# Passage from the cross-attention to the feed-forward of a decoder block: first unit's products inside the drain, later norms and weight splits behind it

## What is computed

```python
x = x + attn(_layernorm(x))            # stage A: differential attention, window 64
x = x + xattn(_layernorm(x), ctx_512)  # stage B: attention to a context, 16 heads
x = x + ffn(_layernorm(x))             # stage C: shared MLP + 16 experts, top 6

# stage C
shared_out = silu_and_mul(xf @ shared_w1.T) @ shared_w2.T
probs = softmax(xf @ gate_w.T)
routing_weights, selected = top_k(probs, 6)
combine = zeros((T, E)).at[arange(T)[:, None], selected].add(routing_weights)
act = silu_and_mul(einsum('th,eoh->teo', xf, w1))
out = einsum('te,tei,ehi->th', combine, act, w2) + shared_out
```

## Time and profile before

| | us |
|---|---|
| three runs | 1419.23, 1417.41, 1419.37 |
| median | 1419.23 |
| the profiled execution: its own time | 1418.07 |
| the profiled execution: span | 1416.2 |
| TensorE busy in the span | 1343.2 (95%) |
| TensorE granted clock, mean | 0.981 |

### The profile page before, as it was taken

The page is one execution under the profiler, slowest core; times in us unless marked ns, Lnnn a source line. Parts: engine busy times, 40 slices in busy tenths (PEclk is TensorE's granted clock), DMA queues, the critical chain, the costliest instruction groups (busy, mean ns, idle before and its releaser), DMA issues.

```text
span 1416.2 us, 28178 instructions
## 1 busy us (share of the span) xinstructions
PE 1343.2 (95%) x10072; PEld 1038.7 (73%) x10072; DVE 850.3 (60%) x1985; ACT 678.0 (48%) x2705; POOL 471.1 (33%) x466
## 2 busy tenths in 40 slices
PE   5899999999999888999999999978999999999998
PEld 4677777877777665576675676646888888888887
DVE  7878778777787666656555655754544343343433
ACT  2676666676666653434444444463333232332322
POOL 3222113112122124545435434551034253443522
PEclk9999999999999989999999999987999999999999
DMA  6011001100011200100101001001026225253230
GB/s 209 23 24 39 16 17 41 29 16 16 16 25 51 75 1 1 72 1 10 63 1 45 27 1 57 1 1 56 32 47 151 42 84 114 41 130 66 46 103 30
DMA packets 29685, 64.59 MB, mean 46 GB/s; under 512 B 6784, under 2 KB 12032, under 8 KB 28288
## 3 DMA queue, kind: packets, MB, share of 16 engines
q1 hardware_dynamic: 29568, 63.05, 16.4%
HBM read 52.42 MB, written 2.23 MB: 39 GB/s over the span
## 4 chain that ended last, share of the span: by engine, by line
PE 72%; issue 12%; DVE 6%; POOL 4%; ACT 4%; DMA 2%; SPq 1%; POOLq 0%; DVEq 0%; ACTq 0%
PE ps L514 30%; PE ps L877 9%; PE ps L800 4%; PE ps L696 4%; PE ps L629 4%; PE ps L661 3%; PE ps L790 3%; PE ps L774 3%; PE ps L782 2%; PE ps L672 2%; POOL ea L1617 2%; PE ps L652 2%; DMA cw<-comb_d 1%; PE ps L569 1%; PE ps L625 1%
## 5 line engine op out<-in xcount | busy, mean ns | idle before, releaser
L1746 POOL TENSOR_TENSOR sg<-sg,cw 128x512 f32<-128x512 f32 x88 | 113.6, 1291 | 278.0 <-ACT sg L1553 268.1
L1357 ACT ACTIVATE pt<-ps 128x512 f32<-128x512 f32 x128 | 76.8, 600 | 245.8 <-PE ps L645 132.0
L1331 DVE TENSOR_TENSOR hh<-ps,sg 128x512 f32<-128x512 f32 x100 | 69.2, 692 | 181.3 <-POOL sg L1746 164.9
L1390 ACT ACTIVATE ea<-ps,negmax 128x64 f32<-128x64 f32 (+1 forms) x512 | 165.4, 347 | 6.0 <-DVE negmax L1083 6.0
L1357 ACT ACTIVATE hhh<-hh 128x512 fp32r<-128x512 f32 x100 | 63.2, 632 | 207.7 <-DVE hh L1331 207.7
L514 PE MATMUL ps<-xnh,wch 128*128 128x512 f32 x400 | 159.4, 399 | 0.5 <-DVE x_sb L1044 0.5
L514 PE MATMUL ps<-xnh,wcl 128*128 128x512 f32 x400 | 159.3, 398 | 0.0
L514 PE MATMUL ps<-xnl,wch 128*128 128x512 f32 x400 | 158.3, 396 | 0.0
L1130 DVE TENSOR_TENSOR qcs<-ps,tabb 128x512 f32<-128x512 f32 x192 | 123.5, 686 | 56.0 <-PE ps L514 55.7
L1617 POOL TENSOR_TENSOR ea<-ea,rden 128x128 f32<-128x128 f32 (+1 forms) x128 | 62.3, 508 | 246.8 <-DVE rden L1039 246.8
L1624 POOL TENSOR_TENSOR eb<-eb,rsum 128x512 f32<-128x512 f32 x64 | 66.7, 1042 | 173.5 <-DVE rsum L1170 173.5
(11 more groups left out here) (148 smaller groups left out, 3436.8 us busy)
## 6 DMA issues: line engine op xcount, KB each, us to landing
raw_w<-in_rawb_dram SPq DMA_DIRECT2D x4, 2432.0 KB, 9.4
kva<-ktmp SPq DMA_DIRECT2D x64, 128.0 KB, 2.3
cw<-comb_d SPq DMA_DIRECT2D x32, 256.0 KB, 5.0
raw_w<-in_rawc_dram SPq DMA_DIRECT2D x4, 1920.0 KB, 7.9
cw<-comb_d SPq DMA_DIRECT2D x16, 224.0 KB, 4.4
raw_a<-in_wqk_dram SPq DMA_DIRECT2D x4, 768.0 KB, 4.8
cw<-comb_d SPq DMA_DIRECT2D x16, 192.0 KB, 6.3
cw<-comb_d SPq DMA_DIRECT2D x16, 160.0 KB, 5.6
```

Source lines behind the costliest of these rows:

```text
L1331: dve.tensor_tensor(hh[:, par, :], bank(C_U[par]), sg[:, par, :], ALU.mult).then_inc(c_h, 1)
L1357: return act.activation(dst, src, ACT.Copy)
L1390: last = act.activation(dst(m, h), src, ACT.Exp, bias=negmax[:, par, i:i + 1], accum_out=sums[:, par, i:i + 1])
L1746: pool.tensor_tensor(sg[:, par, :], sg[:, par, :], cw[:, c % 2, t, :], ALU.mult).then_inc(c_hs, 1)
```

## The change

The first stage C step's gate product moves into drain 1, ahead of the value product, and its up product behind the output product of drain 1 (new functions `c_gate`, `c_up`, cut out of `c_unit`). Norm 9's transposes move from unit 12 to the end of unit 14, norm 10's from drain 0 to step k = 1, norm 11's from k = 0 to k = 3. On DVE the statistics of norm 10 move ahead of an `add_x` in unit 15, `ln_low(9)` to drain 0, `ln_norm(10)` from drain 0 to drain 1, `ln_norm(11)` behind the hidden features of k = 0, and the low halves of norms 10 and 11 to k = 2 and 4. The splits of tiles 3 and 4 move on ACT from unit 15 to k = 8 and 9, and on POOL behind the norms. The logits move from k = 2, 4 to k = 4, 5 and the routing steps on DVE and ACT from k = 2 to 6 to k = 4 to 7. SP's program is the same in both.

```diff
@@ -410,4 +410,3 @@
         B_EXTRA = {("final", 12, 0): [("ln", 8, 0, 2), ("ln", 8, 1, 3)],
-                   ("final", 12, 1): [("ln", 9, 0, 7), ("ln", 9, 1, 2)],
-                   ("drain", 0, 2): [("ln", 10, 0, 2), ("ln", 10, 1, 3)]}
+                   ("final", 14, 2): [("ln", 9, 0, 7), ("ln", 9, 1, 3)]}
@@ -738,4 +737,2 @@
                         if what[0] == "ln":
-                            if what[1:3] == (9, 1):
-                                pe.wait_ge(ln_h, 2 * 8 + 1)
                             if what[1] == 8:
@@ -744,4 +741,3 @@
                                 pe.wait_ge(b_qs, NG * NC)
-                            if drain:
-                                pe.wait_ge(ln_h, 2 * 9 + 2)
+                                pe.wait_ge(ln_h, 2 * 8 + 2)
                             ln_turn(*what[1:])
@@ -788,2 +784,4 @@
                     wait(pe, b_ol, n - 2)
+                    if drain and u == 1:
+                        c_gate(0, 0, 0, 0)
                     for i in range(2):
@@ -802,2 +800,4 @@
                     last.then_inc(b_wo, 1)
+                if drain and u == 1:
+                    c_up(0, 0, 0, 0)
                 slot(2)
@@ -805,2 +805,20 @@
+            def c_gate(g, k, c, t):
+                v = g * (NC * TG) + k
+                if c == 0:
+                    pe.wait_ge(c_lo, g * TG + (t + 1))
+                if isinstance(g, int) and g == 0 and t == 0:
+                    ln_ready(2 * NC + c)
+                wait(pe, c_sg, v - 1)
+                three_pass(bank(C_G[k % 2]), lambda kt: wch[:, t, 128 * kt:128 * (kt + 1)],
+                           lambda kt: wcl[:, t, 128 * kt:128 * (kt + 1)], c).then_inc(c_g, 1)
+            def c_up(g, k, c, t):
+                v = g * (NC * TG) + k
+                wait(pe, c_h, v - 1)
+                three_pass(bank(C_U[k % 2]), lambda kt: wch[:, t, 256 + 128 * kt:384 + 128 * kt],
+                           lambda kt: wcl[:, t, 256 + 128 * kt:384 + 128 * kt], c).then_inc(c_u, 1)
             def c_logits(p, bk):
@@ -866,4 +884,2 @@
-            pe.wait_ge(b_y, NG * UN)
             def c_down(v, par, g, c, t):
@@ -884,20 +900,16 @@
                 v = g * (NC * TG) + k
-                if c == 0:
-                    pe.wait_ge(c_lo, g * TG + (t + 1))
                 first = isinstance(g, int) and g == 0
-                if first and t == 0:
-                    ln_ready(2 * NC + c)
-                wait(pe, c_sg, v - 1)
-                three_pass(bank(C_G[k % 2]), lambda kt: wch[:, t, 128 * kt:128 * (kt + 1)],
-                           lambda kt: wcl[:, t, 128 * kt:128 * (kt + 1)], c).then_inc(c_g, 1)
-                wait(pe, c_h, v - 1)
-                three_pass(bank(C_U[k % 2]), lambda kt: wch[:, t, 256 + 128 * kt:384 + 128 * kt],
-                           lambda kt: wcl[:, t, 256 + 128 * kt:384 + 128 * kt], c).then_inc(c_u, 1)
-                if first and k == 0:
-                    for kt in range(KT):
-                        ln_turn(3 * NC - 1, kt, kt)
+                if not (first and k == 0):
+                    c_gate(g, k, c, t)
+                    c_up(g, k, c, t)
                 if first and k == 1:
+                    pe.wait_ge(b_y, NG * UN)
+                if first and k in (1, 3):
+                    m = 2 * NC + 2 + k // 2
+                    for kt in range(KT):
+                        pe.wait_ge(ln_h, 2 * (m - 1) + kt + 1)
+                        ln_turn(m, kt, C_X[kt])
+                if first and k in (4, 5):
                     pe.wait_ge(ln_h, 3 * NC * KT)
-                if first and k in (2, 4):
-                    c_logits(k // 2 - 1, C_X[k // 2 - 1])
+                    c_logits(k - 4, C_X[k - 4])
                 if first and k in (7, 11):
@@ -905,2 +917,4 @@
                         c_turn((k - 7) // 2 + i, C_X[i])
+                if first and k == 1:
+                    pe.wait_ge(b_ex, NG * UN)
                 if before is not None:
@@ -1171,2 +1185,8 @@
                 slot(1)
+                if final and u == 15:
+                    ln_stats(10)
+                if drain and u == 0:
+                    ln_low(9)
+                if drain and u == 1:
+                    ln_norm(10)
                 if not (first and u < 3):
@@ -1188,10 +1208,2 @@
                     c_zero()
-                if final and u == 13:
-                    ln_low(9)
-                if final and u == 15:
-                    ln_stats(10)
-                if drain and u == 0:
-                    ln_norm(10)
-                if drain and u == 1:
-                    ln_low(10)
                 if drain and u == 2:
@@ -1336,11 +1348,12 @@
                     c_add(v - 1, (c - 1) % NC, None)
-                if first and k == 1:
-                    ln_low(3 * NC - 1)
-                if first and k in (2, 5):
-                    gate_take(k // 3, C_X[k // 3])
-                if first and 2 <= k < 8 and (k - 2) % 3 < 2:
-                    gate((k - 2) // 3, 2 * ((k - 2) % 3))
-                    gate((k - 2) // 3, 2 * ((k - 2) % 3) + 1)
+                if first and k == 0:
+                    ln_norm(3 * NC - 1)
+                if first and k in (2, 4):
+                    ln_low(2 * NC + 1 + k // 2)
+                if first and k in (4, 6):
+                    gate_take(k // 2 - 2, C_X[k // 2 - 2])
+                if first and 4 <= k < 8:
+                    gate(k // 2 - 2, 2 * (k % 2))
+                    gate(k // 2 - 2, 2 * (k % 2) + 1)
-            ln_norm(3 * NC - 1)
             for k, (c, t) in enumerate(C_FIRST):
@@ -1471,6 +1484,4 @@
                             ln_take(*what[1:])
-                    if final and s == 2 and u >= UN - CB:
-                        c_high(0, u - (UN - CB))
-                    if final and (u, s) == (UN - 1, 2):
-                        c_high(0, TG - 1)
+                    if (final and (u, s) in ((13, 2), (15, 2))) or (drain and (u, s) == (0, 2)):
+                        c_high(0, 2 if drain else (u - 13) // 2)
                     if drain:
@@ -1559,7 +1570,9 @@
                 copy(hhh[:, par, :], hh[:, par, :]).then_inc(c_hr, 1)
-                if first and k == 0:
+                if first and k in (1, 3):
                     for kt in range(KT):
-                        ln_take(3 * NC - 1, kt, kt)
-                if first and k in (2, 5):
-                    gate_exp(k // 3)
+                        ln_take(2 * NC + 2 + k // 2, kt, C_X[kt])
+                if first and k in (4, 6):
+                    gate_exp(k // 2 - 2)
+                if first and k in (8, 9):
+                    c_high(0, k - 5)
@@ -1726,14 +1739,16 @@
                     ln_rstd(2 * NC + 1)
-                if u in (12, 13):
-                    ln_low(2 * NC + u - 12)
-                if u in (14, 15):
-                    c_low(0, u - 14)
+                if u == 12:
+                    ln_low(2 * NC)
+                if u == 14:
+                    c_low(0, 0)
                 if u == 15:
                     ln_rstd(2 * NC + 2)
-            for t in range(2, TG):
-                c_low(0, t)
-            ln_low(2 * NC + 2)
+            ln_low(2 * NC + 1)
+            c_low(0, 1)
+            c_low(0, 2)
             ln_rstd(3 * NC - 1)
+            ln_low(2 * NC + 2)
             ln_low(3 * NC - 1)
+            for t in range(SH_N, TG):
+                c_low(0, t)
```

More of the change, by code:

```diff
@@ L1726, in _ @@
                     ln_rstd(2 * NC + 1)
-                if u in (12, 13):
-                    ln_low(2 * NC + u - 12)
-                if u in (14, 15):
-                    c_low(0, u - 14)
+                if u == 12:
+                    ln_low(2 * NC)
+                if u == 14:
+                    c_low(0, 0)
                 if u == 15:
                     ln_rstd(2 * NC + 2)
-            for t in range(2, TG):
+            ln_low(2 * NC + 1)
+            c_low(0, 1)
+            c_low(0, 2)
+            ln_rstd(3 * NC - 1)
+            ln_low(2 * NC + 2)
+            ln_low(3 * NC - 1)
+            for t in range(SH_N, TG):
                 c_low(0, t)
-            ln_low(2 * NC + 2)
-            ln_rstd(3 * NC - 1)
-            ln_low(3 * NC - 1)
             def c_scale(g, c, t):
```

## The result

| | before | after |
|---|---|---|
| median of five runs, us | 1419.23 | 1410.77 |
| lowest and highest, us | 1417.41, 1419.55 | 1407.10, 1411.95 |
| the profiled execution: own time, span, us | 1418.07, 1416.2 | 1407.88, 1406.1 |
| TensorE mean granted clock | 0.981 | 0.991 |

After over before is 0.9937, with a 95% interval of 0.9920 to 0.9954: 8.5 us faster by the medians, 1410.8 where 1408 was forecast. The changed kernel was not timed again beside the experiments. Against it, differences of medians and of ratios can part by some us, so both are given where a reading hangs on them.

What follows compares the result with a forecast made beforehand. Stage C was taken as bound by TensorE, so the passage's losses are never won back. 16.4 (passage) - 3.4 (late load) - 1.7 (clock) = 11.3 us gained, giving 1408; eight in ten: 1402.5 to 1414.

Steps and rivals of the forecast that it cites:

- The passage: Unit 13 to the first down product of stage C: 16.4 us gained, 9.7 of waiting and 6.7 of lower clock.
- the norm: `ln_norm(10)` on DVE in drain 1: two instructions held by 1.8 us, two at 0.4, done at 954.9.
- The clock: TensorE's granted clock: one stretch at the lower level, like that of 998 to 1002, costing 1.7 us.
- that rival: Drain: the clock stays low as before, its 6.7 us are not had, gain 6.3, so 1413; chance 0.16.
- held longer: Drain: each of `ln_norm(10)`'s four instructions held by POOL, last output product 3.2 us later, so 1411; chance 0.09.
- The late load: SP in stage C: next weights' load goes out ahead of chunk 0's stores, routing weights late, 3.4 us given back.
- the slack of 1.35 us: Step k = 12: `hhl` ended at 1038.59, its down product could start at 1039.94; 1.35 us taken off the wait.
- about 1020: Sign of being right: TensorE idle by 2 to 5 us ahead of one down product in stage C at that time.
- the main range: Time of the whole kernel: 1405.5 to 1411 us around the forecast of 1408, given a chance of 0.50.
- unit 13's 1.3 us: Unit 13: without norm 9's copies and a `c_high` ahead of `pt`, the value product starts at 937.1, not 938.4.
- the products in the drain: Drain 1: gate and up product cover `ln_norm(10)` and the last `obl`, ready at 955.7, just inside the up product.
- rows 10: Trace rows: a spread issued 0.4 us behind the 1920 KB load took 7.6 us, the load 8.2; taken for the stores.

## Why the prediction came out right

**The passage: right, mark by mark.** With the 1.54 us added back:

| value product of unit or step | predicted | after + 1.54 |
|---|---|---|
| 13 | 937.1 | 937.1 |
| 14 | 941.05 | 941.1 |
| 15 | 945.7 | 945.8 |
| drain 0 | 948.65 | 948.7 |
| gate product, drain 1 | 951.5 | 951.35 |
| first down product | 961.35 | 961.75 |

The gain is 15.9 for 16.4. The 0.4 of the last mark is the norm, 4.46 us where I took 3.95, which left the `obl` behind it 0.24 us outside its cover, and adds to what follows; the rest is the mark before, which I took from the chain's row, 978.63, and not from PE's, 978.47. The clock held through the passage, so that rival fell; so did "held longer": 4.46 is half a microsecond, not 3.2.

**The late load: right in place and mechanism, mis-sized.** Load at 1009.40 ("about 1010"), landing of the last spread 13.5 us behind it (13.3). That 13.5 met 13.3 is partly luck: the stores had landed 8.35 us behind the load's issue where I took 9.3, and from there to the landing of the last spread it took 5.2 us where I took 4.0. The failed step is the slack of 1.35 us: I set the end of `hhl` against the down product, but that product also waits for the add of the step before, which stands behind `hhl` on DVE. The trace before has it, DVE right behind the last of the earlier trace rows:

```profile
1038.51 1.28 DVE L1321 TENSOR_TENSOR x_sb<-ps,x_sb 128x512 f32<-128x512 f32 x2
```

It ends at 1039.8, and the down product started at 1039.94. The slack was 0.1 us, as three runs then showed. Wait 5.0 for 3.4: of the 1.6 us the slack makes 1.2, and 0.4 comes from the routing weights, by which POOL's product was 5.1 us late and not 4.7. The sign "about 1020" for the wait was loose as well: the prediction's own terms put it at about 1027 (1039.94 - 16.4 + 3.4), and with the 1.54 us added back it stood at 1029.3.

**The clock: 2.1 for 1.7**, at the wait it was tied to, and gone with that wait in both runs that removed it. The size was a guess by one stretch, as the prediction says.

**The sum**: 15.9 - 5.0 - 2.1 = 8.8 by the mechanisms, 11.3 forecast. The median fell by 8.5. The profiled execution shows 10.2 because of 1.5 us ahead of the site. The forecast time, 1408, was 2.8 us low: 1.6 by the wait, 0.4 by the clock and 0.5 in the passage, so most of it in what is given back. The median came out 0.2 us inside the upper end of the main range, 1411; with runs from 1407.10 to 1411.95 it could as well have fallen outside.

**Where the credit inside the passage was wrong.** I gave unit 13's 1.3 us to norm 9's copies and a `c_high` together. The total is right (8.13 to 6.87), but the copies are 0.6 of it, and cost 1.2 two units on; no run took the `c_high` by itself. And the products in the drain, which I had costed as cover, are that and no more.

**Of the two rules.** Stores behind the load landed late, as rows 10 had it: the Trainium skill's order in one queue (DMA: Bandwidth & Descriptors, "Two DMAs through the same engine are not ordered") agrees, 6.5 us behind the load and 1.5 without it. No run put the stores on another queue, so it is not shown whether the order in the queue or the DMA engines' shared time holds them. On the shared ports (SBUF — State Buffer, "Who interferes with whom"), the Trainium skill also says that a DVE instruction with at most one SBUF input stays clear of POOL outside the fast modes, and one with two does not stay clear of a POOL instruction that reads SBUF. The runs agree: `obl` and the add, one input from PSUM, kept 0.42 us beside a split, which reads SBUF; `geq`, both inputs in SBUF, went from 0.29 to 1.86.

## What to carry to other kernels

When a step is moved, list every queue that waits for its semaphore, also in programs that the diff doesn't touch: here one line of SP's list gave back 7 of the 16 us, and reordering it brought them home. Before calling the distance between two rows slack, look for what else the later one waits for, behind the first on the same engine. Work moved under a stall is worth the stall that it covers: price it with the stall's cause gone too, since that may be the cheaper cure.

## What the runs showed of the hardware

- A large transfer delays small ones issued just behind it on the queue: stores of 8 KB landed in 6.5 us behind a load of 1920 KB (7.7 us itself), in 1.5 us without it.
- One DVE instruction of 0.29 us can hold DVE for the whole of a POOL instruction: `geq` took 1.86 us beside POOL's 1.86. Other instructions beside the same kind of split were not held: `obl` and the add, with one input in PSUM, kept 0.42 us. A norm's four instructions took 4.46 us beside two splits and 1.37 without.
- The clock fell or held behind the same gap: behind TensorE's 0.85 us wait for the last `obl` it was 1.00 in one execution and 0.66 over 5 us in another of a kernel with the same drain. A difference of 1.7 us (one such stretch) between single executions therefore says nothing of a kernel, and that is the size of the improvements that could not be seen in the times.
